# A mixture of experts that computes every expert for every token, against one that sorts the tokens to their experts

## The reference

```
shared = (silu(x @ sw1.T) * (x @ sw3.T)) @ sw2.T           # 256 -> 512 -> 256, every token
s      = sigmoid(x @ router_w.T + t_bias)                  # 8 scores for each token
top 2 by s + router_bias; gate = s_chosen / (sum of the two + eps)
routed = sum over the 2 chosen e of gate_e * (gelu(x @ rw1[e].T) @ rw2[e].T)   # 256 -> 128 -> 256
y      = (shared + routed) / 3
```

## Time and profile before

| | |
|---|---|
| three runs, us | 1231.72, 1230.99, 1231.85 (median 1231.72) |
| the profiled execution, us | 1231.89, its span 1229.8 |
| busy, us | PE 1102.4, PEld 847.4, DVE 898.7, ACT 550.1, POOL 246.3 |
| granted clock over the span | 0.99 |
| from the first router product of the mixture to the maximum over y | 804.84 to 1114.41 |

### The profile page before, as it was taken

The page is one execution under the profiler, slowest core; times in us unless marked ns, Lnnn a source line. Parts: engine busy times, 40 slices in busy tenths (PEclk is TensorE's granted clock), DMA queues, the critical chain, the costliest instruction groups (busy, mean ns, idle before and its releaser), DMA issues.

```text
span 1229.8 us, 31887 instructions
## 1 busy us (share of the span) xinstructions
PE 1102.4 (90%) x10420; PEld 847.4 (69%) x10421; DVE 898.7 (73%) x3007; ACT 550.1 (45%) x1743; POOL 246.3 (20%) x285
## 2 busy tenths in 40 slices
PE   6777777877878999999999999789999999996898
PEld 5665665665657888888888888646776567763355
DVE  5676676776776688965555555468898988988887
ACT  4555555555554333333333333362445424444276
POOL 1002112112115675243333333300000000001000
PEclk9999999999999999999999999989999999998999
DMA  7222332332334577444444444241000000000024
GB/s 179 78 71 86 100 94 85 100 98 81 99 96 113 94 168 141 88 73 61 63 62 63 64 64 64 50 124 69 2 1 1 0 1 1 1 1 1 1 34 105
DMA packets 98711, 82.31 MB, mean 67 GB/s; under 512 B 58529, under 2 KB 88354, under 8 KB 98594
## 3 DMA queue, kind: packets, MB, share of 16 engines
q1 hardware_dynamic: 82946, 57.98, 18.6%
q0 software_dynamic: 15648, 22.86, 10.7%
HBM read 41.18 MB, written 33.60 MB: 61 GB/s over the span
## 4 chain that ended last, share of the span: by engine, by line
PE 77%; DVE 10%; ACT 8%; issue 3%; DMA 1%; SPq 0%; POOL 0%; DVEq 0%
PE ps L572 24%; PE ps L1129 17%; PE ps L1139 17%; PE ps L1686 7%; DVE ps L1615 6%; PE ps L1691 4%; ACT work L1539 4%; ACT ps L1534 3%; DVE imax L1008 2%; PE ps L1656 2%; PE ps L917 1%; PE ps L922 1%; PE ps L888 1%; PE ps L1664 1%; DVE W L836 1%
## 5 line engine op out<-in xcount | busy, mean ns | idle before, releaser
L1157 ACT ACTIVATE lane<-ps,b_now 128x256 f32<-128x256 f32 x312 | 147.7, 474 | 260.0 <-PE ps L1129 246.0
L1129 PE MATMUL ps<-lane,W 128*128 128x256 f16 x1872 | 212.8, 274 | 0.9 <-issue 0.8
L1139 PE MATMUL ps<-W,lane 128*128 x1872 | 210.9, 273 | 0.2
L1129 PEld LDWEIGHTS ps<-lane,W 128*128 x1872 | 183.7, 98 | 23.8 <-issue 1.7
L1139 PEld LDWEIGHTS ps<-W,lane 128*128 128x128 f16 x1872 | 182.6, 98 | 22.3 <-issue 0.8
L1686 PE MATMUL ps<-work 128*128 128x16 f16 x2048 | 98.9, 177 | 86.1 <-ACT work L1539 85.5
L1686 PEld LDWEIGHTS ps<-work 128*128 128x128 f16 x2048 | 76.2, 107 | 137.8 <-ACT work L1539 136.4
L572 PE MATMUL ps<-W,work 128*128 128x512 f16 x768 | 168.5, 381 | 0.1
L1298 POOL DMA_INDIRECT results<-lane,dest x78 | 124.7, 1598 | 217.0 <-DVE lane L1212 184.3
L1224 DVE TENSOR_TENSOR lane<-lane 128x256 f16<-128x256 f32 x312 | 133.3, 427 | 10.8
L572 PEld LDWEIGHTS ps<-W,work 128*128 128x128 f16 x768 | 74.8, 98 | 90.1 <-issue 1.9
(11 more groups left out here) (213 smaller groups left out, 1466.7 us busy)
## 6 DMA issues: line engine op xcount, KB each, us to landing
stage<-in_w1T SPq DMA_DIRECT2D x16, 512.0 KB, 3.6
stage<-in_w2T SPq DMA_DIRECT2D x16, 512.0 KB, 4.1
b_now<-in_b SPq DMA_DIRECT2D x39, 128.0 KB
work<-in_zT SPq DMA_DIRECT2D x32, 128.0 KB, 2.1
results<-in_xn SPq DMA_DIRECT2D x32, 128.0 KB
W<-results SPq DMA_DIRECT2D x8, 512.0 KB, 3.8
rows<-work SPq DMA_DIRECT2D x8, 257.0 KB, 5.2
out<-W SPq DMA_DIRECT2D x4, 512.0 KB, 4.0
```

The costliest lines, as they stand in the source:

```text
L1129: last = pe.matmul(ps[:, f % 4, 0:ST], of_e(W1[:, bass.ds(e, 1), a, k, f * P:(f + 1) * P]), xT[:, p, b, k], start=(i == 0 and k == 0), sto ...
L1139: last = pe.matmul(ps[:, 4 + q, 0:D], hid[:, a, f, q * P:(q + 1) * P], of_e(W2[:, bass.ds(e, 1), b, f]), start=(i == 0 and f == 0), stop=( ...
L1157: act.activation(v4[:, f % 4], ps[:, f % 4, 0:ST], ACT.Relu, bias=b1_now[:, p, f:f + 1], scale=A_SCALE / W_SCALE).then_inc(l1_v, 1)
```

## The change

The shared part stays as it is for every token, but the routed part is computed only for the two chosen experts of each token. For that the tokens are sorted in HBM a second time:

- **Routing in four steps of two groups.** `mix_route_op` is a chain of 32 DVE operations on 8x8 scores (two groups at once), and PE counts ranks with nine small products between them (`mix_ranks`). It yields for each token the two rows of the table `mrows` it goes to. Between these operations stand the first 32 units of the shared part, whose banks are now three instead of eight.
- **Rows out.** `mixture_pool` sends each 128 rows of x (high and low half, 1024 bytes, and 4 numbers: token, first expert, gates) twice with an indirect DMA: 64 in all. There are four buffers of such rows (`XBUFS`), so groups 4 to 7 wait in `input_hi` until the DMAs of groups 0 to 3 have landed.
- **A table** of 39 tiles (`mix_table`), filled up with rows of padding by SP. During it and until the rows have landed PE has 12 further shared units.
- **39 tiles of 256 rows.** SP loads rows and weights into four buffers each, rows one tile ahead of the weights (`load_rows_of`, `load_weights_of`, each after a value that SP reads from SBUF). PE transposes tile n+1, does the first layer of tile n, up to one shared unit, and the second layer of tile n-1. ACT copies the transposes, takes Gelu and the high half; DVE the low half, three small operations for the gates and the destinations (six buffers), and the product with the gate. POOL writes each tile with two indirect DMAs that add nothing (`mresults` has a place for each of the two results of each token).
- **The end.** 22 shared units, and for each group a load of 1 MB of routed results, two additions of 1024 elements in each partition and a maximum (`combine`).

The weights of the routed experts go to HBM during the last of the 39 large tiles (`rweights`, 2 MB), and 2 MB of padding rows are copied in HBM at the start of the program. x1 is loaded with two loads in flight. Everything after the maximum over y is the same.

```diff
-U_PAIR = U_OUT + GT
-UNITS = U_PAIR + GT * E // 2
-PRE_UNITS = 1 + DC
-YG = GT * (1 + E)
+ROW_BUFS = 4
+GATE_BUFS = 6
+MIX_OPS = 32
+UNITS = 2 * HSC + GT
+BRIDGE_UNITS = 12
+TILE_UNITS = 30
+LATE = 6
+COMBINE = (0, 1, 2, 6, 3, 4, 5, 7)
+def first_layer(g, w):
+    at = UNITS * g - (GT if g else 0)
...
+        BANKS = 3
+        def unit_bank(v):
+            return 8 - BANKS + v % BANKS
...
+            def mix_ranks(m):
+                flat = m16_m[:].rearrange("p j e -> p (j e)")
+                pe.wait_ge(router_step, MIX_OPS * m + 15)
...
+            def shared(v):
+                g, w = UNIT[v]
+                if v >= BANKS:
+                    pe.wait_ge(unit_read, v - BANKS + 1)
+                if w < 2 * HSC:
+                    c, weights = w // 2, (sw1s, sw3s)[w % 2]
...
-                        reader_done(g, u)
-                        if q == 0:
-                            pe.wait_ge(lo1, HC * g + HSC + 2 * p + 2)
-                        for j in range(2):
-                            last = split_matmul(ps[:, bank_of(u), j * D:(j + 1) * D],
-                                                lambda s, k: hid1[:, s, HSC + 2 * p + j, q * P:(q + 1) * P],
-                                                lambda s, k: rw2s[:, s, 2 * p + j], range(1))
-                        last.then_inc(unit, 1)
...
+            for m in range(STEPS_M):
+                v = STEP_UNITS * m
+                for g in (2 * m, 2 * m + 1):
+                    router(g)
+                for k in range(3):
+                    shared(v + k)
+                mix_ranks(m)
+                for k in range(3, 6):
+                    shared(v + k)
+                for g in (2 * m + 2, 2 * m + 3):
+                    if g < GROUPS:
+                        transposes(g)
+                    shared(v + 4 + g - 2 * m)
+            for v in range(STEPS_M * STEP_UNITS, FIRST_TILE_UNIT):
+                shared(v)
...
+                pe.wait_ge(mT, n + 1)
+                pe.wait_ge(mw_ready[n % ROW_BUFS], 16 * (n // ROW_BUFS) + 16)
+                if n >= 2:
+                    pe.wait_ge(mgelu, n - 1)
...
+                pe.wait_ge(mlo, n + 1)
+                if n >= 2:
+                    pe.wait_ge(mout_set, n - 1)
...
+            for n in range(SLOT_TILES):
+                if n < SLOT_TILES - 1:
+                    tile_transposes(n + 1)
+                tile_first(n)
+                for v in tile_units(n):
+                    shared(v)
+                if n:
+                    tile_second(n - 1)
+            tile_second(SLOT_TILES - 1)
+            for v in range(TAIL_UNIT, UNITS * GROUPS):
+                shared(v)
...
+                if g >= XBUFS:
+                    act.wait_ge(moved[b], 2 * GT * 16 * (g // XBUFS))
...
+            for n in range(SLOT_TILES):
+                if n < SLOT_TILES - 1:
+                    tile_T(n + 1)
+                act.wait_ge(m1_ps, n + 1)
+                if n >= 2:
+                    act.wait_ge(mlo, n - 1)
+                act.activation(mv[:, n % 2], ps[:, 1 + n % 2, 0:ST], ACT.Gelu, scale=1.0 / MIX_SCALE).then_inc(mgelu, 1)
+                act.wait_ge(mgelu, n + 1)
+                if n >= 2:
+                    act.wait_ge(m2_ps, n - 1)
+                act.activation(mhid[:, n % 2, 0], mv[:, n % 2], ACT.Copy, scale=V_SCALE).then_inc(mhi, 1)
+                for v in tile_units(n):
+                    shared(v)
...
+            for m in range(STEPS_M):
+                v = STEP_UNITS * m
+                mix_route_op(dve, m, 0)
+                shared(v)
+                for n in range(1, 9):
+                    mix_route_op(dve, m, n)
+                shared(v + 1)
+                for n in range(9, 15):
+                    mix_route_op(dve, m, n)
+                shared(v + 2)
+                for n in range(15, 28):
+                    mix_route_op(dve, m, n)
+                shared(v + 3)
+                for n in range(28, MIX_OPS):
+                    mix_route_op(dve, m, n)
+                for g in (2 * m + 2, 2 * m + 3):
+                    shared(v + 2 + g - 2 * m)
+                    if g < GROUPS:
+                        input_lo(g)
+                for k in (6, 7):
+                    shared(v + k)
+            mix_table(dve)
+            for v in range(STEPS_M * STEP_UNITS, FIRST_TILE_UNIT):
+                shared(v)
...
+            def tile_gates(n):
+                dve.wait_ge(mrow_in[n % ROW_BUFS], 16 * (n // ROW_BUFS) + 16)
+                if n >= GATE_BUFS:
+                    dve.wait_ge(mstored[n % TILE_BUFS], SQ * 16 * ((n - GATE_BUFS) // TILE_BUFS + 1))
+                dve.scalar_tensor_tensor(mdest[:, b], tail(1), mine, tail(0), ALU.is_equal, ALU.add).then_inc(mdest_set, 1)
+                dve.scalar_tensor_tensor(mmask[:, b], tail(1), mine, tail(3), ALU.is_equal, ALU.mult).then_inc(mgate_step, 1)
+                dve.wait_ge(mgate_step, 2 * n + 1)
+                dve.tensor_tensor(mgate[:, b], mmask[:, b], tail(2), ALU.add).then_inc(mgate_step, 1)
+            def tile_lo(n):
+                dve.wait_ge(mhi, n + 1)
+                dve.scalar_tensor_tensor(mhid[:, n % 2, 1], mv[:, n % 2], V_SCALE, mhid[:, n % 2, 0], ALU.mult,
+                                         ALU.subtract).then_inc(mlo, 1)
+            def tile_out(n):
+                b = n % TILE_BUFS
+                dve.wait_ge(m2_ps, n + 1)
+                dve.wait_ge(mgate_step, 2 * n + 2)
+                if n >= TILE_BUFS:
+                    dve.wait_ge(mstored[b], SQ * 16 * (n // TILE_BUFS))
+                dve.tensor_tensor(mout[:, b], ps[:, 3 + n % 2].rearrange("p (q d) -> p q d", q=SQ),
+                                  mgate[:, n % GATE_BUFS].broadcast_to([P, SQ, D]), ALU.mult).then_inc(mout_set, 1)
+            dve.wait_ge(mtable, 3)
+            tile_gates(0)
+            for n in range(SLOT_TILES):
+                tile_lo(n)
+                for v in tile_units(n):
+                    shared(v)
+                if n < SLOT_TILES - 1:
+                    tile_gates(n + 1)
+                if n:
+                    tile_out(n - 1)
+            tile_out(SLOT_TILES - 1)
+            def combine(at):
+                g, b = COMBINE[at], at % TILE_BUFS
+                yg = y[:, GT * g:GT * g + GT]
+                if g < LATE:
+                    dve.wait_ge(routed_in[b], 16 * (at // TILE_BUFS) + 16)
+                    link(dve, dve.tensor_tensor(yg, yg, routed[b][:, :, 0], ALU.add))
+                else:
+                    dve.wait_ge(unit_read, output_unit(g, GT - 1) + 1)
+                link(dve, dve.tensor_tensor(yg, yg, routed[b][:, :, 1], ALU.add))
+                dve.tensor_reduce(ymax[:, g:g + 1], yg.rearrange("p q d -> p (q d)"), AX.X, ALU.max).then_inc(combined, 1)
+            first_late, last_late = output_unit(LATE, 0), output_unit(GROUPS - 1, 0)
+            for v in range(TAIL_UNIT, first_late):
+                shared(v)
+            for at in range(3):
+                combine(at)
+            for v in range(first_late, first_late + GT):
+                shared(v)
+            combine(3)
+            for n in range(3):
+                for v in range(first_late + GT + 2 * n, first_late + GT + 2 * n + 2):
+                    shared(v)
+                combine(4 + n)
+            for v in range(last_late, UNITS * GROUPS):
+                shared(v)
+            combine(GROUPS - 1)
...
+        def mixture_pool(pool):
+            rows_flat = mrows_d.rearrange("r s n -> (r s) n")
+            for g in range(GROUPS):
+                pool.wait_ge(router_step, MIX_OPS * (g // 2 + 1))
+                pool.wait_ge(xn_lo, g + 1)
+                pool.wait_ge(tok_set, g + 1)
+                for k in range(2):
+                    for q in range(GT):
+                        at = GT * (g % XBUFS) + q
+                        pool.indirect_dma_start(out=rows_flat, in_=xrow[:, g % XBUFS, q], in_offset=None,
+                                                out_offset=bass.IndirectOffsetOnAxis(ap=mslot_of[:, k, at:at + 1], axis=0))\
+                            .then_inc(moved[g % XBUFS], 16)
+            for n in range(SLOT_TILES):
+                b = n % TILE_BUFS
+                pool.wait_ge(mout_set, n + 1)
+                pool.wait_ge(mdest_set, n + 1)
+                for q in range(SQ):
+                    pool.indirect_dma_start(out=mresults_d, in_=mout[:, b, q], in_offset=None,
+                                            out_offset=bass.IndirectOffsetOnAxis(ap=mdest[:, n % GATE_BUFS, q], axis=0))\
+                        .then_inc(mstored[b], 16)
...
+            sp.dma_start(mrows_d[E * REGION:], pads_d[E:]).then_inc(spare_rows, 16)
...
+            sp.dma_start(rweights_d.rearrange("e p n -> p e n"), rweights.rearrange("p (e n) -> p e n", e=E)).then_inc(rw_out, 16)
...
+            for g in range(GROUPS):
+                if g >= 2:
+                    sp.wait_ge(x_in[g % 2], 16 * (g // 2))
                 load_x1(g)
```

(34 more changed lines are left out.)

679 lines of the change are left out of this document (399 added, 280 removed).

## The result

The changed kernel takes 1203.27 us (median of four runs, 1199.73 to 1204.75) against 1231.62 us before on the same chip: ratio 0.9762, 95% interval 0.9742 to 0.9782. Forecast were 1202 us and 1184 to 1232. Timed again later: 1202.84 us, ratio 0.9759 (0.974 to 0.9778).

A forecast was written before the change was run, and what follows sets the result against it. PE was taken to bound the mixture, busy 304.98 of 310 us. Start, routing steps, 39 tiles and end put the maximum at 1084.6 instead of 1114.4: 1231.9 - 29.8 = 1202 us, range 1184 to 1232.

The forecast's parts named there:

- The start: Before the first router: two groups to bring, halve and transpose, +2.7 us; first scores at 808.4 instead of 805.66.
- The steps: Four routing steps with 32 shared units: DVE paces them, 80 us in all; POOL's 64 row DMAs open the tiles.
- rival (e): Routing steps: ACT's wait for landed rows throws each step back 5 us, 1222 us in all; chance 9%.
- The tiles: 39 tiles after the routing: PE slowest at 2.86 us, taken as 3.05 us a tile, 119 us.
- (a): Everything hides: tiles at 2.86 us, a faster end, rows 3 us sooner, 1188 us in all; chance 17%.
- The end: After the tiles: DVE alone on the path from 1043.3, 41.3 us to the maximum at 1084.6.
- what was to be seen: Signs in the mixture: PE busy about 168 us less but 70%, tiles 2.9 to 3.2 us apart.
- (c): POOL's 142 indirect DMAs cost 1.9 us each with the gap, 1265 us in all; chance 10%.
- (b): Tiles wait on transfers or on SP: 3.5 us a tile, +18, 1220 us in all; chance 16%.
- (d): PE's clock stays at the lower level through the tiles, over 1300 us in all; chance 3%.

The follow-up runs named there:

- a1: The changed kernel, unedited, run again on another chip: 1202.84 us, ratio 0.9759 to the kernel before.
- p1: Changed kernel with a POOL fill of 0.53 us behind each of the 64 row DMAs: 1225.41 us, 22.6 us above the unedited one.
- e1: Changed kernel with eight row buffers instead of four, on a slow chip: 1285.41 us, ratio 1.0383 to the kernel before.
- e1b: Changed kernel with eight row buffers instead of four, on another slow chip: 1284.06 us, ratio 1.0382 to the kernel before.
- e4: Changed kernel without shared units in the tile stage, all 30 in the tail, on a slow chip: 1323.58 us, 39.4 above the unedited one there.
- b1: Kernel before with 128 indirect POOL DMAs, which no other work waits for, beside its mixture: 1233.62 us, ratio 1.0011.
- b2: Kernel before with 128 plain DMAs issued by SP, which no other work waits for, beside its mixture: 1233.31 us, ratio 0.9998.
- b3: Kernel before with 64 indirect POOL DMAs, then 128 plain SP DMAs, beside its mixture, on a fast chip: 1234.02 us, ratio 1.0011.

## Why the prediction was right, and where not

| step | forecast | measured (first run; a1) |
|---|---|---|
| first scores | 808.4 | 808.3; 808.4 |
| first row DMA | 821 | 822.5; 822.6 |
| last row DMA out | 903.5 | 910.1; 907.9 |
| first tile | 912.5 | 915.5; 912.9 |
| 39 tiles, to the last product | 119 | 111.7; 112.6 |
| first combination | 1043.3 | 1041.7; 1040.0 |
| maximum | 1084.6 | 1087.45; 1084.6 |

**The start** was right: the second group costs 2.6 to 2.7 us, and the rest is hidden.

**The steps** were right in kind, since POOL's chain opens the tiles, as p1 shows. The chain was 3 to 6 us longer than I had it: a row DMA takes 1.034 us on the mean instead of the 0.985 of the earlier trace rows, 3.1 us over 64, and the chain started 1.5 us late. Most take 0.97; the six that take 1.4 to 2.0 are just those that start while DVE makes a low half of x (L969, both inputs in SBUF), and each ends 0.84 to 0.86 us after that instruction:

```profile
842.37 1.21 DVE L969 SCALAR_TENSOR_TENSOR W<-W 128x1024 f16<-128x1024 f32 x1
842.56 1.87 POOL L1331 DMA_INDIRECT mrows<-W,mslot_of  x1 [0.30 <-issue]
```

So POOL waits there for DVE, which costs this chain some 4 us. The steps themselves were longer than 20 us (21.9, 23.3, 24.0 between their scores), because ACT waited for landed rows for 12.4 us, not the "1 or 2" that I gave it:

```profile
846.10 1.06 ACT L772 ACTIVATE W<-W 128x1024 f16<-128x1024 f32 x1 [10.09 <-DMA mrows<-W,mslot_of]
```

My argument, "the buffer is asked for 20 us after its DMAs began", forgot that ACT comes early: it asks for it as soon as its share of the step is done. That is rival (e)'s mechanism. Its price of 5 us a step did not come, for most of the wait falls where DVE has pairs and outputs in hand, and POOL still has rows to send: it idled 2.6 us in all between its batches (30.3 us before L1331 by the waits, of which 27.7 before the first row).

**The tiles** were the mis-sized term: I added 0.2 us a tile to a floor of 2.86 for imperfect hand-overs, and measured are 2.86 to 2.89. The slack that I counted in each hand-over was enough to hide all of it; (a) was right here. In the timeline a tile with a unit starts 3.05 us after the one before, one without 1.81. POOL needs 2.55 for its two DMAs, close enough to fall behind: its last DMA ends 5.7 us after PE's last product (1032.9 against 1027.2), where I had 3.3 (0.7 and 2.6), and this is 2.4 of the 2.7 us of loss between the tiles and the first combination.

**The end** took 45.7 us from the first combination, 41.3 forecast. The working is right up to the last four units; these took 8.2 us instead of 5.2, because PE had fallen to the lower clock: it had idled for 9.51 us before them, the granted clock from 1078 to 1082 us is 0.50, and the first two reads are 2.6 us apart, where 1.31 is the price of a unit at the full clock. I had put that at "1 to 2 us" and let the tiles' 0.2 pay for it. So the time came out right partly by luck, for errors cancel: 7.3 us too much for the tiles against 3.0 before them, 2.7 behind them and 4.4 at the end that I had too little; the sum is off by 2.8 us in the first profile. In a1 it is 6.4 against 0.4, 2.7 and 3.3, and off by nothing. The forecast time was closer than its working.

**A slip in what was to be seen:** I named 168 us less for PE. The profile has 79 us less (1102.4 to 1023.2): the tiles' own 1.85 us x 39 = 72 come back, as my own sum had it. Of the 17 us that are left the lower clock must take a part (0.82 to 0.93 in three stages, 0.99 before); how much is not worked out here. Nor did PE fall to 70% of the mixture, but to 79 (228 of 289 us).

**The rivals.** (c), POOL's DMAs at 1.6 us: fell, they take 0.972 and 1.034 on the mean beside a DVE that is busy for 69% of the stretch, and 0.975 for the median in p1; L1572, which adds, still takes 1.605 on the same page. This points to the adding, though no run changes it alone. But (c)'s wait of POOL for DVE is real in small, as the six long row DMAs show; it is rare, since DMAs that start beside DVE's reads of PSUM (L996, L1003, L1056) keep their 0.97. The single 1.31 of the earlier trace rows looks like another: it ends 0.87 us after a DVE instruction of 0.69 (L1174, one input, from 438.87) that ran when it started. The Trainium skill ("SBUF — State Buffer", Who interferes with whom), which I had weighed for (c), names two cases, and I had used only the first: DVE's two-port modes, and a DVE instruction with two inputs in SBUF against a GpSimd instruction that reads SBUF. The trace agrees with the second, by the 1.87 us beside L969. (b): fell where the kernel takes 1203; PE is busy for 111.28 of the tiles' 113 us. (d): fell, 0.97.

**What no rival had** is the other kind of chip: 81 us more, of which 77 stand in the mixture, in pauses between what PE ends and what the next engine begins. No row of the profile before shows such a pause. The part of the text that failed there is "each hand-over has a tile or more of slack", taken as a matter of durations alone.

## What stays open

On one chip the kernel loses 77 us in the mixture, and on a second one its edits take as long as on the first. The cause is open. Shown: operations keep their median durations; the loss stands in the stages in which POOL scatters; it does not change when the buffers' waits go (e1, e1b), nor by more than 3.6 us when 39 us of PE's work go (e4); PE finishes and DVE starts up to 11 us later; the waits without a signal are all for PE. Theory S fits most of this, but is not shown: b1, b2, b3 and p1, made to tell it apart from O, all fell to the chip on which there is no delay. In its words, a delay of signals, it does not cover the gaps of up to 1.17 us inside one group's router products, where PE waits for no signal. Two rivals were not tested: that the instructions themselves reach PE and the others late, and that the recording has a part, since every time here comes with a recorded span and clock, and the slow records are the ones that lack signals. Nor do I know what sets the two kinds of chip apart. The run that would tell most is b3 on a slow chip: 30 us or more in its first stretch would speak for S against O, and its second would say whether plain DMAs do it too.

## What to carry to other kernels

Price a stage by its slowest chain and then ask who follows closely: here POOL's indirect DMAs on the path, 1.28 us each and some longer beside DVE's low halves, cost one to one (p1), and moving their start and the uncovered last units, with eight buffers, gave 9.4 us. In this kernel, on the chip of 1203 us, slack of a whole buffer hid the hand-overs, and a term added for them was too much; what was missing was a term for PE, which had just idled and came back at the lower clock.

A kernel that trades engine work for many small DMAs and many signals should be timed on more than one chip before it is called faster: this one is 2.4% faster on one and 3.9% slower on another.

## What I had not expected of the hardware

- Two kinds of chip: 1231.6 to 1233 and 1236.9 to 1238 us for the kernel before, 1203 and 1284 for the changed one, with the same granted clock in the large experts (1.00) and the same median durations.
- 128 indirect DMAs with 16.85 MB beside a PE that is 99% busy cost 0.7 us in all (b1, on the fast kind of chip).
- An indirect DMA that starts while DVE makes a low half from two inputs in SBUF ends 0.84 to 0.86 us after that instruction, up to 1.99 us instead of 0.97.
- An indirect DMA that copies takes POOL 0.97 us and one that adds 1.60, with the same rows of 1 KB; that the adding is what costs is argued.
